# A decoder layer with 32 heads on one core: halved projections beside attention, a new order of the score matmuls, heads copied inside SBUF, and loads in smaller parts

## What is computed

```
x = x + attn(layernorm(x))       # q, k, v, o are "bitnet" linears:
                                 #   y = (x @ sign(W).T) * (mean|W| * scale), guarded against nan and inf
                                 # 32 query heads, 8 key/value heads, head size 16
x = x + ffn(layernorm(x))        # W' = base + mean|w - base| * sign(w - base), 1792 inner features
                                 # silu(x @ W1'.T) * (x @ W3'.T) @ W2'.T
```

## Time and profile before

| | us |
|---|---|
| median of 3 runs | 1049.82 |
| lowest, highest | 1045.49, 1054.92 |
| the profiled execution, its time | 1054.04 |
| its span | 1052.0 |
| TensorE busy | 968.0 |
| VectorE busy | 736.5 |
| ScalarE busy | 538.8 |
| GpSimd busy | 293.1 |

### The profile page before, as it was taken

How to read it: one execution, slowest core, us unless ns; L and a number is a source line. 1 busy time by engine, 2 the same in 40 slices (tenths; PEclk the granted TensorE clock), 3 DMA queues, 4 the chain that set the end, 5 groups by cost and what they waited for, 6 DMA issues and landing times.

```text
span 1052.0 us, 14162 instructions
## 1 busy us (share of the span) xinstructions
PE 968.0 (92%) x4770; PEld 617.9 (59%) x4770; DVE 736.5 (70%) x978; ACT 538.8 (51%) x999; POOL 293.1 (28%) x247
## 2 busy tenths in 40 slices
PE   3588989999999989898889999999999999999997
PEld 2433433344344433333357888888888888888886
DVE  6585867888888787789695558855687557864443
ACT  3426768877897889574684331332223232232221
POOL 3134767566766642210000110101111110011110
PEclk9858998999999999688999999999999999999999
DMA  4535577455754575511494000240003300130001
GB/s 149 149 127 171 158 150 227 127 146 174 224 153 115 170 224 161 179 45 32 151 303 151 12 1 1 80 148 17 0 0 120 124 0 0 45 116 1 0 0 40
DMA packets 81361, 110.24 MB, mean 105 GB/s; under 512 B 10144, under 2 KB 33696, under 8 KB 81312
## 3 DMA queue, kind: packets, MB, share of 16 engines
q1 hardware_dynamic: 79152, 108.04, 33.8%
q10 hardware_dynamic: 2160, 1.58, 0.5%
HBM read 76.29 MB, written 32.78 MB: 104 GB/s over the span
## 4 chain that ended last, share of the span: by engine, by line
PE 70%; DVE 14%; DMA 5%; issue 3%; ACT 3%; SPq 3%; POOL 2%; DVEq 0%; ACTq 0%; POOLq 0%
PE psum L1389 15%; PE psum L1390 15%; PE psum L1391 14%; DVE nmx L994 8%; PE psum L1308 7%; PE psum L1298 7%; PE psum L1282 3%; DMA q_slot<-shift 3%; DVE g_alt L963 2%; PE psum L1319 2%; PE psum L1320 2%; PE psum L1225 1%; PE psum L1226 1%; ACT probs L832 1%; SPq L454 1%
## 5 line engine op out<-in xcount | busy, mean ns | idle before, releaser
L994 DVE TENSOR_REDUCE nmx<-psum 128x2 f32<-128x1024 f32 x256 | 300.9, 1218 | 74.6 <-PE psum L1282 74.3
L832 ACT ACTIVATE probs<-psum 128x512 f32<-128x512 f32 x512 | 276.1, 604 | 77.1 <-PE psum L1298 74.9
L1298 PE MATMUL psum<-q_slot,k_slot 50*128 50x512 f32 x512 | 172.0, 492 | 16.9 <-DMA q_slot<-shift 13.0
L1389 PE MATMUL psum<-fxh,wh 128*128 128x512 f32 x448 | 175.2, 391 | 2.2 <-DVE wl L1152 2.2
L1390 PE MATMUL psum<-fxl,wh 128*128 128x512 f32 x448 | 174.9, 390 | 0.0
L1391 PE MATMUL psum<-fxh,wl 128*128 128x512 f32 x448 | 174.7, 390 | 0.0
L719 POOL CAST dh<-w2T 128x512 fp32r<-128x512 f32 (+1 forms) x56 | 50.7, 906 | 430.1 <-PE psum L1391 393.5
L1298 PEld LDWEIGHTS psum<-q_slot,k_slot 50*128 50x128 f32 x512 | 77.5, 193 | 132.1 <-ACT probs L832 85.6
L1308 PE MATMUL psum<-probs,v_slot 128*32 128x512 f32 x1024 | 146.4, 646 | 0.7 <-ACT probs L832 0.7
L1282 PE MATMUL psum<-k_slot,q_slot 48*128 48x512 f32 x512 | 115.3, 465 | 26.7 <-DVE nmx L994 24.8
L1159 DVE TENSOR_TENSOR gate<-gate,psum 128x512 f32<-128x512 f32 x56 | 38.4, 686 | 133.6 <-PE psum L1391 131.3
(11 more groups left out here) (109 smaller groups left out, 1272.7 us busy)
## 6 DMA issues: line engine op xcount, KB each, us to landing
stage<-in_L_ffn_mean_w_dram SPq DMA_DIRECT2D x84, 256.0 KB, 4.6
q_slot<-q_stack SPq DMA_DIRECT2D x64, 192.0 KB, 3.5
stage<-in_L_ffn_w_dram SPq DMA_DIRECT2D x42, 256.0 KB, 4.8
q_stack<-q_hi SPq DMA_DIRECT2D x32, 256.0 KB
weighted_values<-u_sb SPq DMA_DIRECT2D x32, 256.0 KB, 3.8
k_slot<-k_stack SPq DMA_DIRECT2D x64, 96.0 KB, 3.6
xn<-_attn_hidden_states_dram SPq DMA_DIRECT2D x4, 1024.0 KB, 6.8
q_stack<-q_lo SPq DMA_DIRECT2D x16, 256.0 KB
```

What stands on the lines that cost most here:

```text
L832: nc.scalar.activation(probs[kt][:, j, :], BANK[ring_bank(("score", g, kt, j))], ACT.Exp, scale=HEAD_DIM ** -0.5).then_inc(exp_ok, 1)
L994: v.tensor_reduce(column, pair, AX.X, ALU.max, negate=True).then_inc(s_max, 1)
L1298: mm(BANK[ring_bank(("score", g, kt, j))], k_slot[s][rows, kt * P:(kt + 1) * P], q_slot[s][rows, jj, :], start=True, stop=True).then_inc(t ...
L1389: mm(o, lhs_hi, rhs_hi, start=first, stop=False)
```

## The change

- In attention a slice's order on TensorE becomes: J0, J1, scores, (work beside), scores, J2, J3, weigh, (maxima transposed). The ring has the work beside between J1 and J2, the transposed maxima after J3. ScalarE reads the work beside ahead of J2, and `copy_u` comes after all four exponentials.
- An item beside attention is done in two halves of 256 columns, in two slices one after the other: 8 matmuls and one read of 256 columns in each. The order of items is keys, queries 0, values, queries 1 to 3. Guards come 2 slices after the item's first half, the predicated copy 4 slices after it (before 1 and 3).
- Difference and magnitudes on GpSimd go by parts of 512 columns, one a slice. The six weight DMAs of a tile are issued three in one group and three in the next. Tokens and residual are loaded in halves. The reciprocals' path of sequence 0 and its loads start in the third sequence and are spread over groups; the last four weight tiles are loaded one a group.
- Output projections of sequence 0 are at slices 15, 19, 23, 27 of the last sequence (before 16, 20, 24, 28).
- In the opening, key and value weights come first. The heads of group 0 are copied from `q_hi`, `q_lo` to `q_slot` and `k_slot` directly: 12 DMAs from SyncE and 6 from GpSimd. Items 4 and 5 and the output weights' signs stand among the 14 first `scores`; the statistics of sequence 1 stand after uses 9 to 12 of `maxima`, its means after all 14.
- The output factors are spread by transposing a broadcast column on TensorE and copying twice on ScalarE; a store to DRAM and a load of 512 KB are gone.

```diff
-ITEMS = (KTILE, QT, QT + 1, QT + 2, QT + 3, VTILE)
+ITEMS = (KTILE, QT, VTILE, QT + 1, QT + 2, QT + 3)
-GUARD_LAG, PRED_LAG = 1, 3
-INVERT_AT, ATTENDED_AT, PROJECT_AT, PROJECT_EVERY = 4, 10, 16, 4
-DIFF_AT = tuple(range(1, 112, 8))
-SIGN_LAG, ABS_LAG, SUM_LAG = 2, 5, 8
+GUARD_LAG, PRED_LAG = 2, 4
+INVERT_AT, ATTENDED_AT = 27, 9
+PROJECT_AT = (15, 19, 23, 27)
+DIFF_AT = tuple(range(5, 112, 8))
+SIGN_LAG, SUM_LAG = 2, 6
...
-            ring_users += [("score", g, kt, j) for j in J_ORDER[:3]]
+            ring_users += [("score", g, kt, j) for j in J_ORDER[:2]]
+            if beside(g, kt):
+                ring_users.append(beside(g, kt))
+            ring_users += [("score", g, kt, j) for j in J_ORDER[2:]]
             if kt == 1 and g < LAST_G:
                 ring_users.append(("max", g + 1))
-            if beside(g, kt):
-                ring_users.append(beside(g, kt))
-            ring_users.append(("score", g, kt, J_ORDER[3]))
...
+            elif g % 2 == 1 and g // 2 + 1 < IT:
+                load_difference(g // 2 + 1, 0)
+            elif g % 2 == 0 and g // 2 < IT:
+                load_difference(g // 2, 1)
...
 # ScalarE, a slice
-                if j == J_ORDER[3]:
-                    if kt == 0 and g > 0:
-                        copy_u(g - 1)
-                    if beside(g, kt):
-                        beside_out(beside(g, kt))
+                if j == J_ORDER[2] and beside(g, kt):
+                    beside_out(beside(g, kt))
...
+            if kt == 0 and g > 0:
+                copy_u(g - 1)
...
 # VectorE, before the slices
-        for i in range(TT):
-            token_stats(1, i)
-        token_means(1)
         for nn in range(S_AHEAD):
             maxima(nn)
+            if nn in (1, 3):
+                guard(4 + nn // 2)
+                lo_item(4 + nn // 2)
+            if nn == 4:
+                weight_scales(2)
+                output_scales(slice(OT, WTILES))
             if nn == 8:
                 split_shift(0)
+            if 9 <= nn < 9 + TT:
+                token_stats(1, nn - 9)
+        token_means(1)
...
 # TensorE, an item
-                mm(BANK[bank], signs[:, kt, w], xh[:, kt, :], start=(kt == 0), stop=False)
-                last = mm(BANK[bank], signs[:, kt, w], xl[:, kt, :], start=False, stop=(kt == KT - 1))
+                mm(BANK[bank][:, c], signs[:, kt, w], xh[:, kt, c], start=(kt == 0), stop=False)
+                last = mm(BANK[bank][:, c], signs[:, kt, w], xl[:, kt, c], start=False, stop=(kt == KT - 1))
...
 # TensorE, a slice
             shifted_scores(g, kt, J_ORDER[0])
+            shifted_scores(g, kt, J_ORDER[1])
             if n < S_USES:
                 scores(n)
+            if beside(g, kt):
+                beside_in(beside(g, kt))
+            if n < S_USES:
                 scores(n + 1)
-            shifted_scores(g, kt, J_ORDER[1])
             shifted_scores(g, kt, J_ORDER[2])
+            shifted_scores(g, kt, J_ORDER[3])
...
 # TensorE, before the slices
         for nn in range(S_AHEAD):
             scores(nn)
+            if nn in (1, 3):
+                first_item(4 + nn // 2)
+            if nn == 6:
+                output_signs()
```

More of the change, by code:

```diff
@@ L115, in decoder_layer @@
     fac_row = keep("fac_row", [P, 2, KT, P])
+    sums = keep("sums", [P, P])
     dtot = keep("dtot", [P, 3])
@@ L176, in decoder_layer @@
     o_alt = late("o_alt", [P, SEQ])
-    sums = late("sums", [P, P])
     st2 = late("st2", [P, TT, 6])
@@ L313, in decoder_layer, with loaded, first_heads, first_keys @@
     STORES = 3 * 16
+    def loaded(g):
+        return SLOT_LOADS * (g // 4 + 1) + (FIRST_LOADS - SLOT_LOADS if g % 4 == 0 else 0)
     def stored(b, i):
         return STORES * ((5 * b + i) // Q_RING + 1)
+    def first_heads(eng, part, jj, done):
+        src = (q_hi, q_hi, q_lo)[part][1]
+        for h in range(2):
+            r = HALF * h + HEAD_DIM * part
+            eng.dma_start(q_slot[0][r:r + HEAD_DIM, jj, :].bitcast(FP32),
+                          src[HEAD_DIM * (2 * h + jj):HEAD_DIM * (2 * h + jj + 1)].bitcast(FP32)).then_inc(done, 16)
+    def first_keys(eng, part):
+        src = (q_lo, q_hi, q_hi)[part][0]
+        for h in range(2):
+            r = HALF * h + HEAD_DIM * part
+            eng.dma_start(k_slot[0][r:r + HEAD_DIM, :].bitcast(FP32), src[0:HEAD_DIM].bitcast(FP32)).then_inc(slot_in[0], 16)
     def load_group(eng, g, s, done):
@@ L368, in ring_free @@
             eng.wait_ge(xe_ok, 4 * (which[0] - 1) + which[1] + 1)
+        elif kind == "item" and which[2] == 0:
+            eng.wait_ge(y0_ok, NI * (which[0] - 1) + which[1] + 1)
         elif kind == "item":
@@ L628, in _ @@
         pool.wait_ge(facc_init, 1)
+        pool.wait_ge(qh_ok, 2)
+        for part in range(2):
+            first_heads(nc.gpsimd, part, 1, first_in)
+        pool.wait_ge(ql_ok, 2)
+        first_heads(nc.gpsimd, 2, 1, first_in)
         pool.wait_ge(v_ok, 1)
@@ L805, in beside_out @@
             elif kind == "item":
-                scale_item(b, which[0], bank)
+                scale_item(b, which[0], bank, which[1])
             elif kind == "vT":
@@ L983, in _ @@
             v.tensor_tensor(xl[:, kt, :], BANK[kt], xh[:, kt, :].bitcast(FP32), ALU.subtract).then_inc(xl_ok, 1)
-        for i in range(NI):
-            guard(i)
+        guard(0)
+        lo_item(0)
+        guard(1)
+        lo_item(1)
+        guard(2)
+        guard(3)
+        lo_item(3)
         def maxima(nn):
```

385 lines of the change are left out of this document (231 added, 154 removed).

## The result

| | before | after |
|---|---|---|
| median of 9 runs | 1048.52 | 1062.54 |
| lowest, highest | 1044.14, 1054.92 | 1056.57, 1068.11 |
| the profiled execution | 1054.04 | 1059.59 |
| its span | 1052.0 | 1057.8 |
| its mean granted clock | 0.955 | 0.944 |

The ratio of after to before is 1.0126, with a 95% interval of 1.0092 to 1.0159: 13 us slower. The forecast was 1030, so the sign was wrong. The spans of the two profiled executions differ by only 5.8: the one of before took 5.5 more than its kernel's median, the one of after 3.0 less.

What follows compares the result with a forecast made beforehand. A plain attention slice was taken as bound by a two-engine ring, one PSUM bank too few, not by either engine alone. 11 - 9.5 - 8 - 13.5 - 2 = -22 took the profiled 1054.04 to 1032, median 1030 (1018 to 1040).

Steps and rivals of the forecast that it cites:

- A: Opening and slice 0: plus 11 us (minus 3 to plus 16), as late means make TensorE wait for normalized tokens.
- R1: Rival for the opening: it isn't longer, late means cost nothing net, minus 4 there, 1015 in total; chance 0.18.
- B: Groups 1 to 7: minus 9.5 us (minus 3 to minus 15), as shift waits should mostly go.
- C: Groups 8 to 23: minus 8 us (minus 20 to plus 12), plain slices staying at 2.61, stalls going.
- Where work beside follows it hides: Groups 8 to 23: the weighted values' copy makes the next J0 0.67 later, hidden in 5 of 8 groups.
- What goes is stalls: Groups 8 to 23: long predicated copies (at most 2.9 each) and guards that came late go.
- D: Groups 24 to 31: minus 13.5 us (minus 5 to minus 19), from a spread stall, the clock and earlier projections.
- E: Weights stage: minus 2 us (0 to minus 4), as VectorE can put two tiles together before attention ends.
- R2: Rival for item halves: bound by weight loads, plus 21, so 1050 and no change; chance 0.08.
- R3: Rival for attention slices: ScalarE becomes the ring, plus 33 over 96 slices, so 1062, slower; chance 0.12.
- the ring: Plain attention slice: a cycle over TensorE and ScalarE, one PSUM bank too few, 2.61 us before and after.
- R4: Rival for groups 1 to 7 and 24 to 31: the shift still waits for bulk loads, 1045; chance 0.12.

Runs made afterwards that it cites:

- e1: Changed kernel with the statistics and means of sequence 1 taken after VectorE's seventh maxima: ratio 1.0000 to the kernel before, 1048.37 us.
- e7: e1 with the six weight loads of a tile issued together in one group again: ratio 1.0035 to the kernel before.
- e8: e6 with the six weight loads of a tile issued together in one group again: ratio 0.9976 to the kernel before.
- e6: Changed kernel with the statistics early (e1) and the old order everywhere (e5): ratio 0.9909 to the kernel before.
- e3: Changed kernel with ScalarE's copy of weighted values moved between J1 and J2 of a group's second slice: ratio 1.0155 to the kernel before.
- e15: e6 with GpSimd normalizing the next tokens ahead of the difference and every difference a slice later, no load moved: ratio 0.9850 to the kernel before.
- e14: e6 with only a quarter of the weights of tiles 2 to 13 loaded beside attention, means then wrong: ratio 0.9802 to the kernel before.
- e12: e1 with the old order in the last eight groups alone: ratio 0.9909 to the kernel before.
- e18: e15 with the new order in slices with tokens, an item or values beside them, and products and projections a slice later: ratio 0.9813 to the kernel before.
- e5: Changed kernel with the old order on TensorE, in the ring and on ScalarE: ratio 0.9985 to the kernel before.
- e4: Changed kernel with each item beside attention done whole in the first of its two slices: ratio 1.0182 to the kernel before.
- e10: e9 with the four reciprocal loads issued two in group 24 and two in group 25, ahead of the weight loads: ratio 1.0025 to the kernel before.
- e9: e6 with a group's three weight loads issued right behind the shift, ahead of slots and stores: ratio 0.9993 to the kernel before.

## Why the prediction was wrong

**A was right**, in mechanism and size: +12.5 for +11. Group 1's first shifted score came at 101.4 (said: near 100), and the gap of TensorE was 11.0 (said: about 12; ScalarE's was 12.3), ended by the normalized tokens. (87 + 2.3 + 10 is 99.3, where the working has 99.8.) R1 fell. What the working passed over is that 3.5 us (4.77 in the trace) of VectorE's idle time stood in its own list, ahead of the statistics that made the 11 us; e1 put the one into the other. The change was worth 13 us more with that one move, and a prediction that finds such a hole should say so.

**B was right and too small**: -13.7 for -9.5, since the shift waits went and the clock stayed at 1.00 (0.91 before). The halved loads gave part of that: with six together again these groups took 96.1 in e7 (89.0 in e1) and 96.7 in e8 (91.4 in e6).

**C failed in one term, the stalls**, and a second error was made up for. The undisturbed sequence was forecast well: 100.8 said, 101.6 measured (groups 16 to 23 with group 23's last slice at 2.61). "Where work beside follows it hides" was wrong: the copy of weighted values was charged in 3 of 8 groups, and it costs in the others too: 0.61 in a plain slice (3.22 for 2.61) and 0.53 to 0.57 beside half an item (4.08, 4.02, 4.06 in groups 10, 11, 13, against 3.54, 3.45, 3.53 in e3, where it stands in the second slice). That is about 2.5 us a sequence more than said; the place that e3 tried was no freer. Halves were cheaper than said, 0.69 + 0.94 for two against 1.86, 1.4 a sequence. Two undisturbed sequences are 203.1; the other 6.7 us are stalls that the sum had at nothing. "What goes is stalls" counted what left (the long predicated copies did go: mean 0.77 us instead of 1.22 in groups 8 to 23) but not what came: the second three loads are issued in the group that needs them. GpSimd waited 22.8 us for them from 100 to 430 in the changed kernel, and not at all before. Slices of 5.01 (group 8, 1.3 too long) and 5.27 (group 23, 2.7) came of that; the other 2.8 us are in the two slices around the shift wait of group 14. What such waits cost a whole kernel is seen in e15 (6 us) and e14 (11 us), both on the base of e6.

**D failed most**: +4.8 for -13.5. Its first term, the stall of 7.78, did go, but groups 24 to 26 fell only from 44.7 to 40.3, 4.4 for the 7.5 that were booked, since slices of 4.37 and 4.07 came behind the new stop in group 23. The larger error is in groups 27 to 31: 83.9 for 74.2, so +9.7 where the sum had up to -6. The step "projections a slice earlier, with VectorE's first step never waiting: minus 3", and the clock's "minus 3", took the new order as neutral in the last sequence, because its ring is the same in an undisturbed slice. It is 9.6 us dearer in the last eight groups (e12 against e1, which differ there alone), and e18 shows that the projections' slice earns nothing. What the order does there is known only in part: more of these groups at the lower clock (0.82 for groups 27 to 31 of the changed kernel, 0.95 in e5), for a reason that stays open. One execution says little here: over all the traces the last eight groups took 119.4 to 126.0 in the seven kernels with the new order at the projections, and 107.5 to 121.9 in the twelve changed ones with the old order there, against 118.9 before (the means are 122.8 and 114.6). So without the new order D would probably have had its sign; e5 and e6, at 110.8 and 111.3, are among the better ones.

**E**: 37.0 for 36.5; nothing was gained. FFN's +2.0 (495.8 for 493.8), untouched by the change, stays unexplained in one pair of executions.

**The rivals.** R2 is out (halves at 3.30 and 3.55, and no dearer than whole items by e4). R3 gave the right total for another reason: plain slices stayed at 2.61, and ScalarE wasn't the ring; of its conditions only the copy, in one slice of four, held. R4 was half right: the shift waited less, but the same bytes in the same queue made another consumer wait, which R4 named only for the shift. The slower side got 0.12, on one mechanism; C's own range reached +12, but no chance was given to C and D failing together, and D's range ended at -5.

## What to carry to other kernels

A transfer that is spread to relieve one consumer can take its slack from another: list for each load when it is issued, how long it lands (4 to 8 us here), and when its first reader, GpSimd included, is due; here moving loads lost 3 to 9 us four times (e7 to e10), and moving the readers a slice later gained 2, 6 and 12. An order of instructions that was equal in an undisturbed slice was not equal in groups with stops, so cost a reorder at the work that stops the ring as well as in the slice that doesn't. And where a change puts a wait after work that the same engine could have done in an earlier idle time, look there first: the move in e1 was worth as much as the whole loss.

## What the runs showed of the hardware

- A stop of TensorE of 2.03 us in a stretch at full clock was followed by a whole group at half clock: 16.89 us at a granted 0.51, against 11.25 (e7, e1). What followed the stop was dearer than the stop. It isn't so behind each stop: one of 1.97 us in e9 was followed by 10 us at 1.00.
- Runs of one kernel spread with the granted clock: e12 took 1030.1 at 0.973, and 1038.7 and 1044.6 at 0.960, in three executions. One profile in such a kernel can mislead by 8 us; e5's was 8 below the median of its twelve executions.
- Predicated copies of 512 columns on VectorE took 0.77 us on average in groups 8 to 23 where GpSimd's differences and magnitudes have 512 columns, and 1.22 where they have 1536 (0.72 in the opening). The longest went from 3.60 to 1.25. The copies also stand a slice later after the change, and no run moved the one without the other.
